# First attention of a two-layer block: probabilities transposed by VectorE blocks and SBUF transfers, mask in the VectorE reduction, out projection of four heads summed in PSUM

## The reference

```python
b, s, _ = hidden_states.shape                       # 2, 512, 512
q = einsum('bsh,oh->bso', hidden_states, Wq)        # 32 heads of 128
k, v = ...                                          # 8 heads of 128
q = q * cos + _rotate_half(q) * sin                 # k likewise
scores = einsum('bkgqd,bksd->bkgqs', qg, k) / sqrt(HD)
scores = where(causal, scores, -inf)
attn = softmax(scores, axis=-1)
out = einsum('bkgqs,bksd->bkgqd', attn, v)
return einsum('bso,ho->bsh', out, Wo)
```

## Time and profile before

| | |
|---|---|
| median of 3 runs | 2512.42 us (2512.02 to 2513.49) |
| span of the profiled execution | 2512.5 us, its own time to the same tenth |
| TensorE busy, products / weight loads | 2342.7 us (93%) / 1922.5 us (77%) |
| VectorE, ScalarE, GpSimd busy | 1446.7 (58%), 1353.5 (54%), 1332.7 (53%) |
| DMA | 113.95 MB, mean 45 GB/s |
| first attention | from the start to 877.6 us |

### The profile page before, as it was taken

The page is one execution under the profiler, slowest core; times in us unless marked ns, Lnnn a source line. Parts: engine busy times, 40 slices in busy tenths (PEclk is TensorE's granted clock), DMA queues, the critical chain, the costliest instruction groups (busy, mean ns, idle before and its releaser), DMA issues. The chain is left out here.

```text
span 2512.5 us, 39450 instructions
## 1 busy us (share of the span) xinstructions
PE 2342.7 (93%) x11687; PEld 1922.5 (77%) x11687; DVE 1446.7 (58%) x3094; ACT 1353.5 (54%) x3637; POOL 1332.7 (53%) x1344
## 2 busy tenths in 40 slices
PE   4999999999999854999999999999999999984998
PEld 3888888888888743788888888888888888763887
DVE  4566666666666672456556565665556656665422
ACT  3666666666666443555555555555555555544321
POOL 3777777777787544445444454445544445324310
PEclk9999999999999976999999999999999999996999
DMA  2111111111111022011101111011110111004210
GB/s 77 51 43 56 45 43 46 42 50 50 41 50 38 29 77 84 30 39 38 47 22 43 38 42 42 21 42 38 42 42 25 40 36 30 18 28 134 88 42 26
DMA packets 62176, 113.95 MB, mean 45 GB/s; under 512 B 7088, under 2 KB 8272, under 8 KB 61936
## 3 DMA queue, kind: packets, MB, share of 16 engines
q1 hardware_dynamic: 62064, 112.68, 14.4%
HBM read 106.37 MB, written 6.29 MB: 45 GB/s over the span
## 5 line engine op out<-in xcount | busy, mean ns | idle before, releaser
L671 ACT ACTIVATE l_probs<-l_score,l_negtop 128x512 f32<-128x512 f32 (+3 forms) x512 | 311.1, 608 | 482.2 <-DVE l_negtop L827 481.3
L908 POOL TENSOR_SCALAR l_probs<-l_probs,l_inv 128x512 f32<-128x512 f32 (+3 forms) x512 | 312.6, 613 | 320.4 <-DVE l_inv L824 318.2
L808 DVE TENSOR_TENSOR acc<-l_out,acc 128x512 f32<-128x512 f32 x504 | 344.8, 684 | 215.7 <-PE l_out L202 213.4
L827 DVE TENSOR_REDUCE l_negtop<-l_score 128x1 f32<-128x512 f32 (+3 forms) x512 | 294.9, 576 | 57.7 <-PE l_score L537 49.0
L207 POOL TENSOR_TENSOR l_w_out_lo<-l_stage,l_w_out_hi 128x512 fp32r<-128x512 f32 x128 | 165.3, 1291 | 267.1 <-ACT l_w_out_hi L596 267.1
L680 ACT ACTIVATE l_probsT_hi<-l_turned 128x512 fp32r<-128x512 f32 (+3 forms) x512 | 262.7, 513 | 70.5 <-PE l_turned L567 67.4
L207 DVE TENSOR_TENSOR l_probsT_lo<-l_turned,l_probsT_hi 128x512 fp32r<-128x512 f32 (+3 forms) x512 | 297.1, 580 | 5.9 <-ACT l_probsT_hi L680 3.3
L567 PE MATMUL l_turned<-ident,l_probs 128*128 128x128 f32 x1664 | 267.8, 274 | 7.7 <-POOL l_probs L908 6.6
L567 PEld LDWEIGHTS l_turned<-ident,l_probs 128*128 128x128 f32 x1664 | 205.6, 141 | 66.8 <-POOL l_probs L908 17.0
L200 PE MATMUL l_out<-l_w_out_lo,l_oT_hi 128*128 128x512 f32 x504 | 215.7, 428 | 17.2 <-issue 9.1
L200 PE MATMUL l_score<-l_kT_lo,l_qT_hi 128*128 128x512 f32 (+3 forms) x512 | 216.0, 422 | 8.6 <-POOL l_qT_lo L207 6.1
(11 more groups left out here) (200 smaller groups left out, 5995.8 us busy)
## 6 DMA issues: line engine op xcount, KB each, us to landing
l_stage<-l_wo SPq DMA_DIRECT2D x128, 256.0 KB, 2.6
l_stage<-l_wq SPq DMA_DIRECT2D x96, 256.0 KB, 2.6
l_stage<-l_wk SPq DMA_DIRECT2D x40, 256.0 KB, 2.6
l_stage<-l_wv SPq DMA_DIRECT2D x40, 256.0 KB, 2.6
ffn_w_lo_words<-f_w SPq DMA_DIRECT2D x33, 256.0 KB, 2.8
acc<-x SPq DMA_DIRECT2D x2, 1024.0 KB, 6.6
lin_x<-x SPq DMA_DIRECT2D x2, 1024.0 KB, 6.7
x_kept<-lin_x SPq DMA_DIRECT2D x2, 1024.0 KB, 4.3
```

The source lines that it names most:

```text
L671: act.activation(probs[:, n % NPR, 0:width[t]], score[n % 2][:, 0:width[t]], ACT.Exp, bias=negtop[:, n:n + 1], accum_out=total[:, n:n + 1] ...
L808: dve.tensor_tensor(acc[:, row], out_of(m, j)[:], acc[:, row], ALU.add).then_inc(s_added, 1)
L827: dve.tensor_reduce(negtop[:, n:n + 1], score[n % 2][:, 0:width[n % TB]], AXX, ALU.max, negate=True).then_inc(s_negtop, 1)
L908: pool.tensor_scalar(tile, tile, inv[:, j:j + 1], 1.0, ALU.mult, ALU.mult).then_inc(s_norm, 1)
```

## The change

The first attention gets a function of its own, `grouped_attention`, with its own tables. In it:

- The probabilities are not transposed by TensorE. `turn_blocks` transposes them on VectorE in blocks of 32x32 into `blocks`; once a slot `move` issues 16 transfers of 32 partitions x 4 x 512 B from `blocks` to `moved`, which carry the blocks to their partitions. When they have landed (lags 10 and 11), ScalarE makes `probsT_hi` from `moved` in four chunks of 512, 384, 256 and 128 columns, and VectorE the `lo` over `moved` itself.
- The mask is an operand of the reduction: `tops` adds it to the scores and takes the extreme in one `tensor_tensor_reduce` that writes the masked scores back to PSUM. The identity pass of TensorE goes.
- `pv` uses the `general` banks, at lag 12. The out projection has one PSUM bank for each tile and sums four heads there; `add_rows` adds to `acc` once for four heads (64 adds, not 256).
- `wq` and `wo` are kept for four heads: 10 loads and splits a group, not 18.
- The last group ends 13 steps after its last tile, not 8.

```diff
@@ -276,6 +276,581 @@
...
+NORM_LAG, BLOCK_LAG, MOVE_LAG, LAND_LAG, PV_LAG, OUT_LAG = 1, 2, 5, 10, 12, 13
+END0 = TILES + OUT_LAG
+PER_MOVE = TB * TB * 16
+USES0 = ([(4 * s - 3, ("q", s)) for s in range(1, SLOTS + 1)]
+         + [(n, (kind, b)) for b, at in ((1, (6, 10, 15)), (2, (18, 22, 27))) for kind, n in zip(("k", "v", "vt"), at)]
+         + [((4 * s + PV_LAG) % TILES, ("pv", s - SLOTS * (4 * s + PV_LAG >= TILES))) for s in range(SLOTS)])
+LOADS0 = ([(4 * h + 1, ("wo", h, 0)) for h in range(GH)] + [(7, ("wk", 0, 1)), (11, ("wv", 0, 1))]
+          + [(4 * h + 15, ("wq", h, 1)) for h in range(GH)])
+FIRST_LOADS0 = [("wk", 0, 0), ("wv", 0, 0)] + [("wq", h, 0) for h in range(GH)]
...
+        out_bank = p.banks(ctx, "l0_out", TB)
...
+        NPR = 4
+        probs = sb("probs", [P, NPR, S])
+        blocks = sb("blocks", [P, 2, TB, TB, P])
+        with ExitStack() as early:
+            moved = p.sb(early, "l0_moved", [P, 2, TB, TB, P])
+        probsT_lo = sb("probsT_lo", [P, 2, TB, TB, P], F32R)
+        probsT_hi = sb("probsT_hi", [P, TB, TB, P], F32R)
...
+            def move(m, slot):
+                wait_past(sp, s_block, m, TILES, TB * (slot + 1))
+                sp.nop(nofuse=True)
+                if not (m.first and slot < 2):
+                    sp.wait_ge(s_bank, m.done(("pv", slot - 2)))
+                else:
+                    sp.wait_ge(s_clear, 1)
+                for g in range(TB):
+                    for c in range(TB):
+                        sp.dma_start(moved[32 * c:32 * c + 32, slot % 2, :, g],
+                                     blocks[32 * g:32 * g + 32, slot % 2, :, c]).then_inc(s_move[slot % 2], 16)
...
+                for n in m.steps():
+                    for x in m.loads_at.get(n, []):
+                        k = m.loads.index(x)
+                        load(k, m.i + x[2], x, m.load_start() + k - 1)
+                    slot = m.slot_at(n, MOVE_LAG)
+                    if slot is not None:
+                        move(m, slot)
...
+                if kind == "pv":
+                    wait_past(pe, s_land_lo, m, TILES, TB * (j + 1))
+                    b, h = divmod(j % SLOTS, GH)
+                    if h == 0:
+                        pe.wait_ge(s_free, m.done(("vt", b)))
+                    for k in range(TB):
+                        seen = slice(k * 32, P)
+                        right = Split(probsT_hi[:, k, :, seen], probsT_lo[:, j % 2, k, :, seen])
+                        last = product(nc, by_quarter(bank[:])[:, :, seen], v[:, b, k * HD:(k + 1) * HD], right,
+                                       k == 0, k == TB - 1)
...
+                b, h = divmod(slot, GH)
+                if t == 0:
+                    pe.wait_ge(s_free, m.done(("pv", slot)))
+                    if b >= 0:
+                        pe.wait_ge(s_w, m.loaded("wo", h))
+                if h == 0:
+                    wait_past(pe, s_added, m, B * TB, TB * (b - 1) + t + 1)
+                last = product(nc, out_bank[t][:], oT[:, slot % 2, t * P:(t + 1) * P], w_out[:, h], h == 0, h == GH - 1)
+                last.then_inc(s_out, 1)
...
+            def body(m):
+                for n in m.steps():
+                    if n < TILES:
+                        slot, t = divmod(n, TB)
+                        if t == 0:
+                            pe.wait_ge(s_rope_lo, m.done(("q", slot), of_qk))
+                        wait_past(pe, s_exp, m, TILES, n - 1)
+                        last = product(nc, score[n % 2][:, 0:width[t]], qT[:, slot % 2, t * P:(t + 1) * P],
+                                       kT[:, slot // GH, 0:width[t]])
+                        last.then_inc(s_score, 1)
+                    if m.lagged(n - OUT_LAG):
+                        project(m, *divmod(n - OUT_LAG, TB))
+                    for x in m.uses_at.get(n, []):
+                        bank_use(x, m, range(C // 2, C) if halves(x, n) else range(C))
+                    for x in m.uses_at.get(n + 1, []):
+                        if n + 1 < TILES and halves(x, n + 1):
+                            bank_use(x, m, range(C // 2))
...
+            def exponentials(m, n):
+                t = n % TB
+                act.wait_ge(s_negtop, m.i * TILES + n + 1)
+                wait_past(act, s_block, m, TILES, n - NPR + 1)
+                act.activation(probs[:, n % NPR, 0:width[t]], score[n % 2][:, 0:width[t]], ACT.Exp,
+                               bias=negtop[:, n:n + 1], scale=-1.0, accum_out=total[:, n:n + 1]).then_inc(s_exp, 1)
+            def landed_hi(m, slot, k):
+                if k == 0:
+                    wait_past(act, s_move[slot % 2], m, SLOTS // 2 * PER_MOVE, (slot // 2 + 1) * PER_MOVE)
+                seen = slice(k * 32, P)
+                act.activation(probsT_hi[:, k, :, seen], moved[:, slot % 2, k, :, seen], ACT.Copy)\
+                    .then_inc(s_land_hi, 1)
...
+            def body(m):
+                for n in m.steps():
+                    if n < TILES:
+                        exponentials(m, n)
+                    for slot, k in landing_chunks(n, m):
+                        landed_hi(m, slot, k)
+                    for x in m.uses_at.get(n - 1, []):
+                        if x[0] in QK:
+                            rope_hi(x, m)
+                    for x in m.loads_at.get(n, []):
+                        work(x, m, m.loads.index(x))
+                    for x in m.uses_at.get(n, []):
+                        if of_turned(x):
+                            bank_hi(x, m)
+                        elif x[0] in QK:
+                            rope_swap(x, m)
...
+            def tops(m, n):
+                w = width[n % TB]
+                dve.wait_ge(s_score, m.i * TILES + n + 1)
+                dve.nop(nofuse=True)
+                dve.tensor_tensor_reduce(out=score[n % 2][:, 0:w], in0=score[n % 2][:, 0:w], in1=mask[:, S - w:S],
+                                         scale=-1.0, scalar=3.0e38, op0=ALU.add, op1=ALU.min,
+                                         accum_out=negtop[:, n:n + 1]).then_inc(s_negtop, 1)
...
+            def turn_blocks(m, n):
+                slot, t = divmod(n, TB)
+                wait_past(dve, s_norm, m, TILES, n + 1)
+                if t == 0:
+                    wait_past(dve, s_move[slot % 2], m, SLOTS // 2 * PER_MOVE, slot // 2 * PER_MOVE)
+                if m.first and n == 0:
+                    dve.wait_ge(s_clear, 1)
+                w = width[t]
+                to = blocks[:, slot % 2].rearrange("p k c x -> p (k c) x")[:, 0:w // 32, 32 * t:32 * t + 32]
+                dve.transpose(to, probs[:, n % NPR, 0:w]).then_inc(s_block, 1)
...
+            def landed_lo(m, slot, k):
+                wait_past(dve, s_land_hi, m, TILES, TB * slot + k + 1)
+                seen = slice(k * 32, P)
+                rest(dve, probsT_lo[:, slot % 2, k, :, seen], moved[:, slot % 2, k, :, seen], probsT_hi[:, k, :, seen])\
+                    .then_inc(s_land_lo, 1)
...
+            def add_rows(m, b, t):
+                wait_past(dve, s_out, m, TILES, TB * (b * GH + GH - 1) + t + 1)
+                row = b % B * TB + t
+                dve.tensor_tensor(acc[:, row], out_bank[t][:], acc[:, row], ALU.add).then_inc(s_added, 1)
...
+            def body(m):
+                for n in m.steps():
+                    if m.lagged(n - NORM_LAG):
+                        j = (n - NORM_LAG) % TILES
+                        wait_past(dve, s_exp, m, TILES, n - NORM_LAG + 1)
+                        dve.reciprocal(inv[:, j:j + 1], total[:, j:j + 1]).then_inc(s_inv, 1)
+                    if n < TILES:
+                        tops(m, n)
+                    for slot, k in landing_chunks(n, m):
+                        landed_lo(m, slot, k)
+                    if m.lagged(n - BLOCK_LAG):
+                        turn_blocks(m, n - BLOCK_LAG)
+                    slot, t = divmod(n - OUT_LAG, TB)
+                    if m.lagged(n - OUT_LAG) and slot % GH == GH - 1:
+                        add_rows(m, slot // GH, t)
+                    for x in m.uses_at.get(n, []):
+                        bank_use(x, m)
...
@@ -1518,7 +2093,7 @@
-        attention_phase(p, ctx, 0, xT, acc, ident, half, x_rows)
+        grouped_attention(p, ctx, xT, acc, ident, half, x_rows)
```

337 lines of the change are left out of this document (added).

## The result

The changed kernel takes 2877.85 us (median of 4 runs, 2869.35 to 2885.25) against 2512.94 us for the kernel before on the same chip: a ratio of 1.1451, with a 95% interval of 1.1429 to 1.1473. It is 365 us slower. The forecast was 2825 us, the range 2630 to 2960.

What follows compares the result with a forecast made beforehand. TensorE's bound would give way to a closed round of waits: 14.2 us, 14.9 with k and v, 15.5 with GpSimd's holds, 17.5 with low clock. 64 x (17.5 - 12.6) = +314 on 2512: 2825 us, range 2630 to 2960.

Steps and rivals of the forecast that it cites:

- a closed round of hand-offs: First attention: TensorE, ScalarE and VectorE wait on each other in a loop that cannot run ahead, 14.2 us a head.
- the bands given: First attention in the new profile: TensorE busy share 60 to 75%, its granted clock between 0.6 and 0.9.
- Which wait closes the round: First attention: TensorE's next pv waits for VectorE's last lo half of the landed blocks, up to some us a head.
- The alternation of VectorE and ScalarE: Round's part outside TensorE: swap and multiply 1.9 us, step 2 3.2, step 3 2.5, handoffs 0.4 for the whole round.
- TensorE's relief: Ten transposes a head leave TensorE, 1.4 us, and four mask products, 0.5 us: 10.6 us of 12.5 are left.
- Rival 2: First attention: TensorE stays the bound, the round hides, only 1.9 us a head count; faster, 2390 us; chance 0.10.
- Transfers at nothing: Sixteen transfers a head, 0.33 us each to issue on SyncE, about 8 us to landing, covered by a five-step lag.
- Rival 3: Sixteen transfers do not overlap and land late: over 3800 us, or above 2960 if partly overlapped; chance 0.07.
- GpSimd against VectorE: VectorE's lo halves, now reading SBUF twice, are held by GpSimd instructions: 0.6 us a head, ends 0 and 2.
- The clock: TensorE's idle gap in every head lowers its clock: 2.0 us a head, ends 0 and 5.1.
- Block transposes and row tops: VectorE in step 2: block transpose of 128 columns 0.2 us, tops of 384 columns 0.55, reading the accumulator 0.1.

Runs made afterwards that it cites:

- e3: Changed kernel with the step-3 weight load issued ahead of the sixteen transfers, and landing, pv and out projection one step earlier: 2782.34 us.
- e7: Changed kernel with the step-3 weight load issued ahead of the sixteen transfers, and q one step earlier: 2782.67 us.
- e1: Changed kernel with SyncE issuing the step-3 weight load in step 1, ahead of the sixteen transfers; nothing else changed: 2858.38 us.
- e5: Kernel before with the mask part alone: no mask product on TensorE, VectorE adds the mask while taking row tops: 2499.63 us against 2514.19.
- e10: Changed kernel with four transfers a head of 128 partitions for sixteen of 32, same bytes, no block changing its partition: 2850.38 us.
- e9: Changed kernel with ScalarE making the hi halves of landed blocks ahead of the step's exponential, not behind it: 2872.65 us.
- e12: Kernel of e11 with q's hi half on ScalarE and its lo half on GpSimd one step later: 2724.26 us.
- e6: Changed kernel with the second multiply and the add of q's and k's rotation on VectorE instead of GpSimd: 2927.51 us.
- e11: Kernel of e7 with ScalarE making the hi halves of landed blocks ahead of the exponential: 2745.55 us.

## Why the prediction held, and which of its steps did not

The direction, the range and the kind of cause held: a closed round of hand-offs, no engine that bounds. TensorE's share (71 to 74%) and its clock (0.82 to 0.85) lie in the bands given, and the 512-column exponentials are 18.0 us apart on the average where 17.5 were forecast. Part of this agreement is luck: TensorE is idle for 4.8 us a head where almost 5 were forecast, but the chain that sets this was not in the sum; it only happens to be about as long as the one that was. Counted on TensorE alone, as an estimate from these traces, a head is 12.8 us before, less some 1.0 for transposes and mask, plus 4.5 for q's lo, 0.3 for the bank of v and 1.9 of low clock: 18.5, and 18.2 were measured. The forecast's 17.5 is lower mainly by a relief that was taken almost 1 us too large.

- **Which wait closes the round.** This step failed, though the number held. I wrote that the next pv waits for its last lo. The score of 128 columns waits first, for q's lo half on GpSimd; pv comes 2.1 us of TensorE work later, and its lo halves are done by then (623.56, pv at 625.29). The alternation of VectorE and ScalarE was sized well: 1.9 + 3.2 + 2.5 = 7.6 us without handoffs, against 7.74 from the swap's start to the last lo's end. But the chain on GpSimd beside it, which I did not add up, is as long (7.4 us from the swap to the score) and ends in a place that has the score and out, 2.1 us at the low pitch, in its round. By the alternation alone pv could have started 1.7 us earlier. e3 and e7, which take most of that wait away, gained 1.9 and 1.5 us a head in this stage, 0.3 of it by e1's edit. That the alternation, nearly as long, keeps the rest is what I take from this; e7's waits for a bank are a rival that no run separates from it.
- **TensorE's relief.** Too large. For the mask 0.5 us was priced from the time of a weight load, 0.12 per product; e5 shows 0.23 for the four. The ten transposes were taken at 0.14 each, but they overlap: the four from 301.03 are followed by the next product at 301.38, three from 311.06 at 311.31, two from 306.88 at 307.04. That is 0.8 for ten and not 1.4. Rival 2, with TensorE still the bound, would so have stood near 2450 us and not 2390.
- **Transfers at nothing.** The landing was hidden, as forecast: no hi half of a landed block waits for a DMA in these 900 us. The issue was not 0.33 but 0.64 us, and I had not looked at what stands behind sixteen issues in SyncE's queue: the weight load, with ScalarE's in-order queue behind it. In this order of steps that costs 19 us (e1), and 28 with what else sixteen issues cost over four (e10). Rival 3's serial landing did not come: issues are 0.64 us apart and each lands 2.0 us after its own, so three are under way at once. The estimate of 2.15 us for one transfer goes by a fit that the Trainium skill's page DMA: Bandwidth & Descriptors gives in the section Anatomy of one DMA — SWDGE (gpsimd) path for transfers issued from GpSimd; for these, issued from SyncE, the trace's 2.0 is near it, and the 3.2 of e10's 256 KB is further off (2.6 by the fit, as an estimate). By the same page's section Rules for kernel authors, transfers to disjoint partition halves serialize; taken so that one starts when the last has landed, this would have made 3470 us, and no trace here shows such a serial order.
- **GpSimd against VectorE.** I took 0.6 us a head for held lo halves. In the changed kernel these are hardly held (733, 546, 455 and 285 ns, before 686, 546, 414 and 280 for 512, 384, 256 and 128 columns). GpSimd's norm is, by 0.83 us, in the very chain that TensorE waits for. The size was right, the victim was the other engine, and e9 shows the upper end of 2 as real.
- **The clock.** Priced at 2.0 a head; heads pay 1.9 on the average, and taking most of it away gave 0.66. It lies in part on a score and an out that my round did not hold. The upper end that I gave, 5.1, comes to 4.9 by the pitches that I used; nothing rests on it.
- **Block transposes and row tops.** 299 ns for 128 columns, where 0.2 was taken. The Trainium skill's page VectorE: DVE Perf Modes, section The three transpose paths, has 311 for bf16: the trace, in float32, is close to it. The mask costs the row tops 0.01 us, the read of the accumulator 139 ns.

The fastest version of the new stage, e12, leaves 2724 us, 211 more than before, 193 of them in the first attention. What the rest consists of was not taken apart further: TensorE is busy for 77% of that stage, at a granted clock of 0.92.

## What to carry to other kernels

Before work is taken from the engine that bounds a stage, add up every chain that starts and ends at that engine, on each of the others, in the order of their queues; where two chains are nearly as long, a repair of one moves the wait to the other, as e6, e9 and e11 show in part. Price a wait over a whole turn of the pattern and not from one head: the 1.2 us of e1's theory came in a quarter of the heads only. When small transfers are added to a queue, ask what is issued behind them and what stands behind that on the engine that waits for it: the same late load cost 0.3 us a head in one order and over 4 in another. And compare the stage and not only the whole: e3 and e7 are equal in total, while their first attentions differ by 24 us. Of a change in several parts, time each alone where it can stand alone: here the one part that is local to a step was a gain.
